# Second experts' weight sets loaded in halves, and three tiles projected ahead of the second attention

## What is computed

```python
x = x + tanh(g_xattn[0]) * _L0_xattn_ref(_layernorm(x), ctx_1024, ctx_1024, ...)
x = x + tanh(g_ffn[0])   * _L0_ffn_ref(_layernorm(x), ...)            # 8 experts, top 2
x = x + tanh(g_xattn[1]) * _L1_xattn_ref(_layernorm(x), ctx_1024, ctx_1024, fside, Wq, Wk, Wv, Wo)
x = x + tanh(g_ffn[1])   * _L1_ffn_ref(_layernorm(x), ...)            # 16 slots, 16 experts
# _L1_xattn_ref, 16 heads:
q, k, v = query @ Wq.T, ctx @ Wk.T, ctx @ Wv.T
out = softmax(q k^T / 4 + bias) v @ Wo.T
# _L1_ffn_ref: slots attend to the tokens; each slot goes through its own expert; tokens attend to the slots
o = q + mha(slot_query, x, x);  h = layernorm(o)
y = (silu(h @ W1 + b1) * silu(h @ Wg + bg)) @ W2 + b2                 # per expert, 256 -> 1024 -> 256
out = mha(x, o + y, o + y)
```

## Time and profile before

| | us |
|---|---|
| median of three runs | 1308.04 |
| the profiled execution, whole | 1310.88 |
| its span | 1309.1 |
| TensorE busy | 1268.9 |
| VectorE busy | 881.8 |
| ScalarE busy | 795.5 |
| GpSimd busy | 747.3 |

### The profile page before, as it was taken

The page is one execution under the profiler, slowest core; times in us unless marked ns, Lnnn a source line. Parts: engine busy times, 40 slices in busy tenths (PEclk is TensorE's granted clock), DMA queues, the critical chain, the costliest instruction groups (busy, mean ns, idle before and its releaser), DMA issues.

```text
span 1309.1 us, 38203 instructions
## 1 busy us (share of the span) xinstructions
PE 1268.9 (97%) x14755; PEld 1133.8 (87%) x14755; DVE 881.8 (67%) x2364; ACT 795.5 (61%) x1739; POOL 747.3 (57%) x835
## 2 busy tenths in 40 slices
PE   9999999998999999999999988999999999999897
PEld 8898888886999999999999967899999998655576
DVE  5888888876566556655564048999999997321386
ACT  5676676654777777777775436665566665423453
POOL 2578888754877787777773054566666643000131
PEclk9999999999999999999999989999999999999999
DMA  6675565633777777777767512621111111599712
GB/s 225 231 257 175 193 207 172 218 131 117 258 221 221 239 216 225 217 231 231 220 213 278 232 45 66 229 93 51 53 51 55 53 61 66 223 428 426 296 64 68
DMA packets 103891, 237.51 MB, mean 181 GB/s; under 512 B 8992, under 2 KB 86176, under 8 KB 91296
## 3 DMA queue, kind: packets, MB, share of 16 engines
q1 hardware_dynamic: 97568, 218.29, 48.7%
q0 software_dynamic: 6144, 16.79, 4.0%
HBM read 174.22 MB, written 60.82 MB: 180 GB/s over the span
## 4 chain that ended last, share of the span: by engine, by line
PE 89%; DVE 4%; DMA 3%; issue 2%; ACT 1%; POOL 1%; DVEq 0%; ACTq 0%; SPq 0%; PEldq 0%; POOLq 0%
PE ps L2140 14%; PE psT L2125 7%; PE ps L714 6%; PE psS L691 5%; PE ps L1084 5%; PE psT L700 4%; PE ps L1026 4%; PE ps L2125 4%; PE psS L2125 4%; PE ps L1009 2%; PE ps L1043 2%; PE ps L953 2%; PE psT L706 2%; DMA arena<-wset_dram 2%; PE ps L2381 2%
## 5 line engine op out<-in xcount | busy, mean ns | idle before, releaser
L2093 POOL TENSOR_TENSOR wb_lo<-arena,wb_hi 128x2048 fp32r<-128x2048 f32 x64 | 296.7, 4637 | 92.0 <-ACT wb_hi L2216 92.0
L2140 PE MATMUL ps<-wb_hi,hT_hi 128*128 128x256 f32 x528 | 151.7, 287 | 0.0
L700 PE MATMUL psT<-arena 32*128 32x128 f32 x2048 | 149.4, 283 | 0.4 <-ACT arena L1256 0.4
L2140 PE MATMUL ps<-wb_lo,hT_hi 128*128 128x256 f32 x528 | 147.7, 280 | 0.0
L2140 PE MATMUL ps<-wb_hi,hT_lo 128*128 128x256 f32 x528 | 147.6, 280 | 0.0
L691 PE MATMUL psS<-arena 32*128 32x256 f32 x1024 | 139.7, 389 | 0.8 <-ACT arena L1333 0.4
L2216 ACT CAST wb_hi<-arena 128x1024 fp32r<-128x1024 f32 x128 | 130.7, 1045 | 4.5 <-DMA arena<-w_dram 4.3
L700 PEld LDWEIGHTS psT<-arena 32*128 32x128 f32 x2048 | 124.6, 186 | 1.7 <-issue 1.2
L1700 POOL TENSOR_TENSOR arena<-arena,eps_sb 128x1 f32<-128x1 f32 x94 | 23.7, 252 | 149.7 <-DVE arena L1571 106.5
L2281 DVE TENSOR_TENSOR arena<-ps,arena 128x512 f32<-128x512 f32 (+1 forms) x39 | 25.4, 651 | 121.5 <-PE ps L2140 81.1
L1713 POOL DMA_INDIRECT arena<-xs_rows,slot_i x64 | 64.4, 1007 | 69.3 <-DMA xs_rows<-arena 54.3
(11 more groups left out here) (508 smaller groups left out, 3862.4 us busy)
## 6 DMA issues: line engine op xcount, KB each, us to landing
arena<-wset_dram SPq DMA_DIRECT2D x24, 2048.0 KB, 16.0
xs_rows<-arena SPq DMA_DIRECT2D x33, 1024.0 KB, 8.8
arena<-w_dram SPq DMA_DIRECT2D x32, 1028.0 KB, 5.9
arena<-w_dram SPq DMA_DIRECT2D x32, 1024.0 KB, 5.9
arena<-w_dram SPq DMA_DIRECT2D x7, 2052.0 KB, 13.3
w_sb<-xs_rows SPq DMA_DIRECT2D x33, 256.0 KB, 2.7
xs_rows<-arena SPq DMA_DIRECT2D x33, 256.0 KB, 5.5
arena<-ctxT_dram SPq DMA_DIRECT2D x63, 128.0 KB, 4.3
```

Of the source, the lines that this page charges most:

```text
L700: nc.tensor.matmul(psT[:, b, j * P:(j + 1) * P], kbd_[p, (k - 1) % NK, c, par, :], qT[p, (k - 1) % 3, c, :], start=j == 0, stop=False, ski ...
L2093: nc.gpsimd.tensor_tensor(wb_lo[:, u % 2, part], wb_raw[:, u % 2, part], wb_hi[:, u % 2, part], ALU.subtract).then_inc(w_g.sem, 1)
L2140: last = nc.tensor.matmul(ps[5][:, t * D:(t + 1) * D], hp[:, f, t * P:(t + 1) * P], wp[:, f, :], start=f == 0 and t == 0 and n == 0, stop= ...
```

## The change

1. `LATE` is 3: one more tile (tile 10) is projected ahead. Its keys are computed ahead of the loop, its values in step 0 between the two halves of the scores. `ctx_first` becomes 11. SP loads set 3, whose place holds the stash of the late tiles, at step 11.
2. The constant products ahead of the loop go from eight to two, those late in step 0 from eight to three, and two times two are added: in step -1 ahead of the query projection, and at the start of step 0.
3. ScalarE writes the three high parts ahead of the early tiles, in the order o1, v1, dv, with a wait for the first experts' last output ahead of dv. POOL writes the low parts of o1 and dv ahead of its first gather, that of v1 in step 1 behind a gather.
4. The weight sets move in halves of 1 MB. There are thirteen places for halves: the twelve of before and one in `w_sb[:, 4:8]`, the place of the second attention's weights. Waits, `set_used` and loads go by halves; the host lays each set out as two contiguous halves of every partition's row.
5. The queries of pairs 3 and 5 are projected in two parts with other work between them, and `normalised(0)` comes ahead of the queries of pair 5.
6. In the last group the table load comes behind `queries_out` and the copy of `ugT`.

The diff, cut to its core:

```diff
-LATE = 2
+LATE = 3
...
+        HALF = 4 * F1 // 2
+        HALVES = 12 * (E1 // 4)
+        extra = 2 * SETS
+        def half_place(i):
+            return i if i <= extra else (i - 1) % extra
+        def half_at(i):
+            p = half_place(i)
+            if p == extra:
+                rows = w_sb[:, 4:8].rearrange("p n c d -> p (n c d)")
+            else:
+                rows = set_at(p // 2).rearrange("p e f -> p (e f)")[:, p % 2 * HALF:(p % 2 + 1) * HALF]
+            return rows.rearrange("p (e f) -> p e f", e=4)
...
-        late_bank = (1, 2)
+        late_bank = (1, 2, 4)
...
 sync, attention:
+                    if not A and 5 <= k < 4 + EARLY_SETS:
+                        sp.dma_start(set_at(k - 5)..., a["wset"][k - 5]).then_inc(ld_set[k - 5], 16)
+                    if not A and k == ctx_first:
                         sp.wait_ge(kv_a.sem, kv_a.at(ctx_first - 1, "V"))
+                        sp.dma_start(set_at(EARLY_SETS - 1)..., a["wset"][EARLY_SETS - 1])...
...
 tensor, attention:
+                def constant_products(n, bank):
+                    for _ in range(n):
+                        nc.tensor.matmul(ps[bank][:, :], ident_b[:, :], ident_b[:, None, :].to_broadcast([P, 4, P]),
+                                         start=True, stop=True)
...
-                    for n in range(LATE):
-                        (keys and values of tile n)
-                    for _ in range(8):
-                        nc.tensor.matmul(ps[4][:, :], ident_b[:, :], ...)
+                    for n in range(LATE - 1):
+                        late_keys(n)
+                        late_values(n)
+                    late_keys(LATE - 1)
+                    constant_products(2, 0)
                 for k in steps:
                     if not A and k == 0:
-                        pe.wait_ge(stash_a, STASH + LATE)
+                        constant_products(2, 7)
+                        pe.wait_ge(stash_a, STASH + LATE - 1)
...
+                    if not A and k == -1:
+                        constant_products(2, 0)
+                    if not A and k == 0:
+                        late_values(LATE - 1)
                     scores(k, 1)
...
                     if not A and k == 0:
-                        for _ in range(8):
-                            nc.tensor.matmul(ps[4][:, :], ident_b[:, :], ...)
+                        constant_products(3, 7)
...
 scalar, attention:
+                    for name in parts:
+                        if name == "dv":
+                            act.wait_ge(m0_last["y"].sem, m0_last["y"].at(UNITS - 1, "y"))
+                        nc.scalar.copy(split[name][0][:, :, :], w[name]).then_inc(hi_a.sem, 1)
                     for i in range(early): (as before)
-                    for name in parts:
-                        nc.scalar.copy(split[name][0][:, :, :], w[name]).then_inc(hi_a.sem, 1)
...
 gpsimd, attention:
                 if not A:
+                    rest_of("o1")
+                    rest_of("dv")
                     (wait for the first experts' rows, gather(0), gather(1))
                 for k in steps:
                     (gather(k + 3))
+                    if not A and k == 1:
+                        pool.wait_ge(kv_p.sem, kv_p.at(early - 1, "V"))
+                        pool.wait_ge(stash_p, STASH + LATE)
+                        rest_of("v1")
...
 sync, moe1:
-                for n in range(EARLY_SETS + 1, 6 * T):
-                    if n >= SETS:
-                        sp.wait_ge(set_used, n - SETS + 1)
-                    sp.dma_start(set_at(n)..., a["wset"][n]).then_inc(ld_set[n % SETS], 16)
+                for i in range(2 * (EARLY_SETS + 1), HALVES):
+                    if i > extra:
+                        sp.wait_ge(set_used, half_freed(i))
+                    sp.dma_start(half_at(i)..., a["wset"][i // 2, :, i % 2 * HALF:(i % 2 + 1) * HALF])\
+                        .then_inc(half_landed(i)[0], 16)
...
+            def half_freed(i):
+                return i - extra if i < 2 * extra + 1 else i - extra + 1
...
 tensor, moe1:
-                queries(pe, 3, 7)
+                queries(pe, 3, 7, (0,))
                 pe.wait_ge(ld_slots, 16)
                 pe.wait_ge(*a1_last["sums"])
                 slots_out(0)
+                queries(pe, 3, 7, (1,))
                 pe.wait_ge(q_a.sem, q_a.at(2, "q"))
                 queries(pe, 4, 6)
                 gain_and_bias(0)
+                normalised(0)
                 pe.wait_ge(q_a.sem, q_a.at(3, "q"))
-                queries(pe, 5, 7)
-                normalised(0)
+                queries(pe, 5, 7, (0,))
...
-                            pe.wait_ge(ld_set[n % SETS], 16 * (n // SETS + 1))
                             for h in range(2):
+                                pe.wait_ge(*half_landed(2 * n + h))
                                 (four matmuls)
+                                if h == 0:
+                                    last.then_inc(set_used, 1)
...
+                            if mat == 0 and c == 0 and t == 0:
+                                queries(pe, 5, 7, (1,))
...
 scalar, moe1:
                     if t + 1 == T:
-                        nc.scalar.activation(table[:, :], ones[:, 0:1], ACT.Exp)
                         queries_out(act, EARLY_PAIRS + 3 * t, 1)
                     (copy of ugT)
+                    if t + 1 == T:
+                        nc.scalar.activation(table[:, :], ones[:, 0:1], ACT.Exp)
```

More of the change, by code:

```diff
@@ L399, in build, with queries @@
         ld_ring, ring_ready, first_hi = sem("ld_ring"), sem("ring_ready"), sem("first_hi")
-        def queries(pe, i, bank):
-            for m in range(C):
+        def queries(pe, i, bank, parts=(0, 1)):
+            for m in parts:
                 for c in range(C):
@@ L406, in queries @@
                                             x_all[:, 2 * i:2 * i + 2, c * P:(c + 1) * P], start=c == 0, stop=c == C - 1)
-            last.then_inc(q_p.sem, 1)
+            if parts[-1] == C - 1:
+                last.then_inc(q_p.sem, 1)
         def queries_out(act, i, bank):
@@ L1228, in scalar @@
                         values(i, early_bank[i])
[L1229 to L1233 removed]
+                    for n in range(LATE - 1):
+                        late_away(n)
                 for k in steps:
@@ L1294, in scalar @@
                         nc.scalar.copy(xT.rearrange("p c t -> p (c t)"), ps[5][:, 0:D]).then_inc(pre_a.sem, 1)
+                    if not A and k == 0:
+                        late_away(LATE - 1)
                     if not A and valid(k - 2):
@@ L2835, in arrange @@
         "slotT": f[p + "slot_query"][0].T.reshape(C, P, NS).transpose(1, 0, 2).reshape(P, -1),
-        "slots": slots, "wset": np.stack(sets),
+        "slots": slots, "wset": np.stack(sets).reshape(-1, P, 4, 2, F1 // 2).transpose(0, 1, 3, 2, 4).reshape(-1, P, 4 * F1),
         "x": f["x"], "ctxT": f["ctx_1024"].reshape(B, P, C, P).transpose(0, 3, 2, 1).reshape(B, P, C * P),
```

82 lines of the change are left out of this document (49 added, 33 removed).

## The result

The changed kernel takes 1301.72 us (median of 6 runs, 1299.96 to 1304.13), the kernel before on the same chip 1308.38 us (6 runs, 1306.98 to 1309.13). The ratio is 0.9947, 95% interval 0.9927 to 0.9966: 6.7 us faster. The forecast was 1300.3 us, range 1298.2 to 1304.2, with 0.87 on faster.

A forecast was written before the change was run, and what follows sets the result against it. TensorE, busy 1268.9 of 1309.1 us with 89% of the chain, was taken to bound the kernel. Terms 3.6 + 1.4 + 0.5 + 2.2 = 7.7 us off the median 1308.04 gave 1300.3 us, range 1298.2 to 1304.2.

The forecast's parts named there:

- Constants and clock (3.6 us): Second attention's opening: at full clock, the transpose of tile 0's maxima starts at 773.4 instead of 777.10, 3.6 us gained.
- Low parts off the loop (1.4 us): Second attention, steps 1 and 2: VectorE's casts fall from 1.03 and 0.74 to 0.17 us, 1.4 us gained.
- One more tile ahead (0.5 us): Second attention, step 9: tile 10's keys and values leave it; 10.82 us becomes 10.2 to 10.4, 0.5 us gained.
- Halves and second experts (2.2 us): Second experts: waits of 1.89, 0.3 and 0.5 us go, 0.5 us new idle time at the opening; 2.2 us gained.
- the first weight product starts at 1131.05, not 1131.50: Second experts' opening: earlier start with half a pair of queries and bias behind the normalised row; half pair returns later.
- the slack of 2.7 us: Second experts' end: last half lands at 1222.0, wanted at about 1224.7; holds until a half takes 2.53 us, not 2.46.
- (c): Rival, second experts: halves stream less well; at 353 GB/s, 2.97 us per half, the kernel takes 1315.5 us; chance 0.04.
- 1318.7: Second experts' weight stream: estimated kernel time in us if halves moved at the skill's 341 GB/s.
- (a): Rival, second attention's opening: the clock falls anyway, a little later; 2.8 us less gain, 1303.1 us; chance 0.12.
- (b): Rival: second experts give nothing, a wait for a half or the opening's row chain replacing the old; 1302.5 us; chance 0.09.
- (d): Rival, second attention: with fewer constants the clock falls and stays down for the following two steps; 1309.8 us; chance 0.03.

The follow-up runs named there:

- run 11: Changed kernel with eight constant products in step 0 instead of three; 1301.94 us, ratio 0.9961 to the kernel before.
- run 1: Kernel before without the eight constant products of step 0, nothing else; 1311.06 us, ratio 1.0003 to the kernel before.
- run 2: Kernel before with only the making of the high and low weight parts moved ahead; 1307.87 us, ratio 0.9975 to the kernel before.
- run 3: Kernel before with only the second experts' part (halves, split queries, earlier normalised(0), later table load); 1309.80 us, ratio 0.9998 to the kernel before.
- run 8: Changed kernel with tile 10's values projected ahead of the loop, not in step 0; 1303.52 us, ratio 0.9973 to the kernel before.
- run 4: Changed kernel without the two times two new constant products in steps -1 and 0; 1305.88 us, ratio 0.9960 to the kernel before.
- three groups: Follow-up runs 1 to 4, 5 to 8 and 9 to 12, each group on one chip together with the kernel before.
- run 9: Changed kernel with two tiles projected ahead of the loop instead of three; 1302.14 us, ratio 0.9961 to the kernel before.
- run 5: Changed kernel measured again, nothing changed; 1301.99 us, ratio 0.9953 to the kernel before.
- run 6: Changed kernel with before's order in the second experts' opening (queries undivided, normalised(0) later); 1298.62 us, ratio 0.9930 to the kernel before.
- run 7: Changed kernel with gain_and_bias(0) right behind slots_out(0), ahead of the queries; 1300.17 us, ratio 0.9936 to the kernel before.
- run 10: Changed kernel with twelve places for halves, the thirteenth left out; 1303.58 us, ratio 0.9977 to the kernel before.
- run 12: Changed kernel with the last group's table load back where the kernel before had it; 1302.07 us, ratio 0.9962 to the kernel before.

## Why the prediction was right, point by point

**Constants and clock (3.6 us): right in the profile, too much for the median.** From the first key projection ahead of the loop to the transpose of tile 0's maxima it takes 19.03 us instead of 22.97, 3.9 us less. The clock stayed at 1.00, and run 11 shows that this, not the number of constants, is the gain. All profiles together carry the term: with the opening of before the clock fell there in all four (before, runs 1 to 3, for 3.4 to 17.1 us), with the changed opening in one of ten (run 8, whose gap is open again). Which of the fills does it is less clear: run 4 doesn't show that the four new constants are needed. What I missed is that the fall differs from execution to execution. I took the profiled execution's fall (6.8 us at half clock) off the median. But of the 87 runs of before in the three groups 19 have a mean clock of 0.999, which leaves room for at most 3.9 us at half clock (1305 x 0.0015 x 2) in the whole execution. In the third group these are ten of 34; they took 1304.3 to 1306.9 us, and those at 0.993 to 0.995 took 1310.6 to 1311.5. The typical run of before has 0.996 or 0.997, which does leave room for the 6.8 us, so it is not shown that the median lacks them. In the second group, where both kernels ran, the runs at 0.999 or above have medians of 1305.2 and 1301.9 us: 3.4 us of gain. Behind the memset it is 8.7 between the profiled executions, and 5.6 to 6.7 between medians.

**Low parts off the loop (1.4 us): right, 1.9.** Between the transposes the steps 1 and 2 gain 0.85 and 0.79 us and step 3 another 0.2; run 2 gives 1.7 by itself. The first gather follows 0.15 us behind dv's low part and starts 2.19 us behind the memset, where it was 2.15: 0.04 late, as allowed for. v1's low part lies beside a reduction of VectorE that reads PSUM, which still takes 1.22 us.

**One more tile ahead (0.5 us): right**, 0.6 (run 9); step 9 gained 0.8 in all, the rest being the effect that follows.

**Not foreseen: 0.8 us in steps 4 to 8.** Each is 0.1 to 0.3 us shorter. I found where, not why. In a step TensorE computes the first half of the scores and the turned scores of the last tile in alternation (L710 and L719, matmuls of 32 rows). Timeline of the changed kernel in step 9, then of run 4's kernel in the same step:

```profile
845.40 0.39 PE L697 MATMUL psS<-fs,mine 32*128 32x512 bf16 x2
...
845.84 0.38 PE L710 MATMUL psS<-arena 32*128 32x256 f32 x2
845.85 0.39 PE L719 MATMUL psT<-arena 32*128 32x128 f32 x4
...
846.41 0.39 PE L725 MATMUL psT<-mT,pick 32*128 32x128 bf16 x8
```

```profile
850.04 0.51 PE L697 MATMUL psS<-fs,mine 32*128 32x512 bf16 x2
...
850.61 0.37 PE L710 MATMUL psS<-arena 32*128 32x256 f32 x1
850.67 0.29 PE L719 MATMUL psT<-arena 32*128 32x128 f32 x2
...
851.22 0.40 PE L725 MATMUL psT<-mT,pick 32*128 32x128 bf16 x8
```

In the first the matmuls go in pairs and the block lasts 1.01 us from L697 to L725; in the second the two of a pair start one after the other, and it lasts 1.18. In the steps 5 to 8 of before the same block lasted 1.61, 1.21, 1.01 (but began 0.3 us late) and 1.07 us, in those of the changed kernel always 1.01. Step 8, from second reduction to second reduction, takes 10.03 to 10.05 us in the profiles of runs 5 to 12, which have the new constants, and 10.15 to 10.43 in those of runs 1 to 4, which have not, and which all ran on one chip. Whether the chip or the constants put the pairs in step was not told apart: it stays open, and so does whether the new constants are worth these 0.8 us.

**Halves and second experts (2.2 us): the term that was mis-sized, 1.0.** The failing step is the one for the opening: "the first weight product starts at 1131.05, not 1131.50". It starts 0.62 us later against the sums, not 0.45 earlier. I followed the row chain through VectorE and POOL and let TensorE's part of it (`gain_and_bias(0)`, behind one and a half pairs of queries) run along; it ended the wait. Runs 6 and 7 show it: with before's order the part gives 2.8 us, with `gain_and_bias(0)` first 1.8. Of the rest, the last set's wait is gone (1.89), the table load's too (0.52, run 12). The slack held, but for most of it that was luck. From the fourth half on the halves land 2.54 us apart (34 of them from 1128.58 to 1214.78), not 2.46; I had written that the slack of 2.7 us is used up at 2.53. The stream also started later than forecast, and the last half landed 101.3 us behind the start of the sums, not 98.9. That 1.7 us were left all the same is because TensorE wanted it 1.45 us later than I had it, 1.07 of them by the late opening. In run 6, where neither the stream nor TensorE starts as late, 0.5 us are left. Without the thirteenth place it would not have held (run 10).

**The rivals.** (c), halves that stream less well: the window of the halves shows 414 GB/s at a share of 1.00, against 427 for sets of 2 MB, 3% less: true in kind, and small enough to stay hidden, with 0.5 us of slack left in run 6. The Trainium skill ("DMA: Bandwidth & Descriptors", Bandwidth, Measured) gives 341 GB/s for transfers of 1 MB issued from GpSimd; with several queued at once from SP this trace shows 414, so here the page's figure doesn't bind. By the prediction's own terms that figure gives an estimate of 1319.2 us (107.6 - 86 - 2.7 on top of 1300.3), not the 1318.7 it states. (a), a clock that falls anyway, did not happen in the opening of the changed kernel's two profiled executions and did in run 8's. (b) came half true: the row chain of the opening took half the gain back. (d) was true of the kernel before without its constants (run 1), not of the changed kernel, where the gaps were filled as well.

That the sum came out close is in part luck, since its errors cancel. Within the profiled executions it had 0.3 and 0.5 us too little in the opening's two terms, missed some 1.3 us of gain in the loop, and had 1.2 us too much for the second experts; together that is 8.6 us where 7.7 were forecast. The medians differ by 2 to 3 us less than the profiled executions do. Of the 4.0 us in the first comparison (10.7 against 6.7) 2.0 lie ahead of the memset, in unchanged code; what the rest is, no run shows.

## What to carry to other kernels

Before a half-clock stretch of one profile is priced, look at the recorded mean clock of many runs: here 19 of 87 runs had no room for it, so its worth differs from run to run. Products without use that stand behind a wait gave nothing when they were taken out alone; they could be cut together with filling the wait ahead of them, best with work that has to be done anyway. When a chain is split between engines to start something earlier, follow it through every engine's queue, the one that is "busy anyway" above all: the piece of it that stands behind other work there sets the end.

## What the runs showed of the hardware

- Two executions with the same work and the same idle time on TensorE (4.35 and 4.34 us busy of 5.40) got different clocks behind it: 1.00 in one, 0.51 for 3.4 us in the other.
- On one chip the runs' spread is mostly that: over 34 runs of one kernel the time goes with the mean clock, 1304.3 us at 0.999 to 1311.5 at 0.993. Between chips it is not: at 0.999 the same kernel took 1304.3 to 1306.9 us on one and 1307.5 to 1308.6 on another.
- Stretches at half clock stand at places whose code is the same in all kernels: in the first attention in six of the fourteen profiles (3.4 or 6.8 us), in the last stage in four.
- A 16-column cast beside a POOL instruction of 1.25 us took 0.40 to 1.03 us, without it 0.17.
- Transfers of 1 MB, several of them queued, ran at 414 GB/s over 86 us with the 16 DMA engines full; sets of 2 MB at 427.
